# A DLRM forward pass: samples taken in pairs of 64-sample units, one unit in each half of the partitions, and which engine copies and which one fetches

## What is computed

```python
x = relu(dense_features @ W0 + b0)        # 13 -> 512
x = relu(x @ W1 + b1)                     # 512 -> 256
dense_out = relu(x @ W2 + b2)             # 256 -> 64
emb = tables[f, sparse_features[:, f]]    # (2048, 26, 64)
gram = einsum('bid,bjd->bij', emb, emb)
interact = gram[:, TRIU_I, TRIU_J]        # 325 products for each sample
y = concatenate([dense_out, interact], 1) @ Wt + bt   # 389 -> 256
```

## Time and profile before

| | before |
|---|---|
| time, median of 3 runs | 537.5 us (534.24, 537.5, 538.75) |
| profiled execution, its own time | 535.61 us |
| its span, first to last instruction | 533.8 us |
| PE busy (matmuls) | 345.1 us, 65% |
| DVE busy | 206.8 us, 39% |
| ACT busy | 203.7 us, 38% |
| POOL busy | 389.7 us, 73% |
| gathers on POOL | 407, 956 ns each |
| mean granted TensorE clock | 0.76 of full speed |

### The profile page before, as it was taken

The page is one execution under the profiler, slowest core; times in us unless marked ns, Lnnn a source line. Parts: engine busy times, 40 slices in busy tenths (PEclk is TensorE's granted clock), DMA queues, the critical chain, the costliest instruction groups (busy, mean ns, idle before and its releaser), DMA issues.

```text
span 533.8 us, 8006 instructions
## 1 busy us (share of the span) xinstructions
PE 345.1 (65%) x1744; PEld 285.4 (53%) x1744; DVE 206.8 (39%) x648; ACT 203.7 (38%) x637; POOL 389.7 (73%) x414
## 2 busy tenths in 40 slices
PE   2067854895846965658747786369854487617975
PEld 1055743674635854537636665257643376516864
DVE  6432344334324343244443342432451425314353
ACT  2023444345224453144432452433541436313462
POOL 6777777777777777777777777777777777777760
PEclk9555887769767788677877697685895869757699
DMA  5214112221122212221212211222212221122110
GB/s 101 46 28 91 27 28 32 33 38 28 27 38 38 28 27 29 38 37 28 29 26 38 39 27 30 38 28 37 28 28 37 38 30 26 28 38 35 27 26 21
DMA packets 23182, 18.66 MB, mean 35 GB/s; under 512 B 12775, under 2 KB 16585, under 8 KB 23116
## 3 DMA queue, kind: packets, MB, share of 16 engines
q0 software_dynamic: 13024, 13.36, 17.8%
q1 hardware_dynamic: 6612, 2.52, 2.2%
q10 hardware_dynamic: 3498, 2.26, 1.4%
HBM read 15.20 MB, written 2.10 MB: 32 GB/s over the span
## 4 chain that ended last, share of the span: by engine, by line
POOL 72%; issue 23%; PE 1%; DVE 1%; DMA 1%; POOLq 0%
POOL emb L283 72%; PE mlp_ps L573 1%; DVE gram L198 1%; DMA emb<-in_L_rec_tables_dram,row_idx 1%; DMA raw_idx<-n_r_sparse_features_dram 0%; PE gram_ps L560 0%; POOLq L79 0%; PE rowsT_ps L543 0%; POOLq L278 0%; DVE out_sb L372 0%; DVE embT L184 0%; DVE wrap L313 0%; DVE row_idx L323 0%; DVE wrapped L317 0%; DVE capped L314 0%
## 5 line engine op out<-in xcount | busy, mean ns | idle before, releaser
L283 POOL DMA_INDIRECT emb<-in_L_rec_tables_dram,row_idx x407 | 388.9, 956 | 127.5 <-issue 123.8
L198 ACT COPY gram<-gram_ps 32x48 f32<-32x48 f32 (+1 forms) x512 | 122.9, 240 | 151.0 <-PE gram_ps L560 145.2
L198 DVE COPY gram<-gram_ps 32x48 f32<-32x48 f32 (+1 forms) x512 | 122.2, 239 | 124.6 <-PE gram_ps L560 117.7
L560 PEld LDWEIGHTS gram_ps<-embT 128*128 128x128 f32 x1024 | 144.5, 229 | 17.2 <-issue 9.4
L560 PE MATMUL gram_ps<-embT 128*128 128x100 f32 x1024 | 148.5, 312 | 4.1 <-DVE embT L184 4.1
L543 PE MATMUL rowsT_ps<-ident,emb 128*128 128x128 f32 (+1 forms) x215 | 49.5, 341 | 157.0 <-DMA emb<-in_L_rec_tables_dram,row_idx 135.6
L184 DVE COPY embT<-rowsT_ps 64x512 f32<-64x512 f32 (+2 forms) x96 | 65.0, 689 | 154.2 <-PE rowsT_ps L543 153.8
L543 PEld LDWEIGHTS rowsT_ps<-ident,emb 128*128 128x128 f32 (+1 forms) x215 | 28.1, 163 | 175.5 <-DMA emb<-in_L_rec_tables_dram,row_idx 129.8
L184 ACT COPY embT<-rowsT_ps 64x512 f32<-64x512 f32 x64 | 53.4, 861 | 109.1 <-PE rowsT_ps L543 108.6
L573 PE MATMUL mlp_ps<-w_gram,gram 128*128 128x256 f32 x224 | 72.3, 485 | 1.9 <-DVE gram L198 1.9
L573 PEld LDWEIGHTS mlp_ps<-w_gram,gram 128*128 128x128 f32 x224 | 57.3, 260 | 14.3 <-DVE gram L198 2.3
(11 more groups left out here) (28 smaller groups left out, 39.8 us busy)
## 6 DMA issues: line engine op xcount, KB each, us to landing
by_hand<-in_L_rec_tables_dram SPq DMA_DIRECT2D x1152, 0.2 KB
emb<-in_L_rec_tables_dram,row_idx POOLq DMA_INDIRECT x407, 2.7
out_dram<-out_sb ACTq DMA_DIRECT2D x16, 128.0 KB, 1.9
w_gram<-w_tri SPq DMA_DIRECT2D x3, 192.0 KB
w_sb<-in_L_rec_W_dram SPq DMA_DIRECT2D x1, 512.0 KB
raw_idx<-n_r_sparse_features_dram SPq DMA_DIRECT2D x2, 182.0 KB, 3.9
w_gram<-w_tri SPq DMA_DIRECT2D x1, 224.0 KB
x_sb<-in_r_dense_features_dram ACTq DMA_DIRECT2D x1, 104.0 KB, 2.8
```

Of the source, the lines that this page charges most:

```text
L198: last = copy(gram[FP * g:FP * (g + 1), q, t0:NS, c0 + a0 * SQ + s:c0 + a1 * SQ:SQ], gram_ps[FP * s:FP * (s + 1), a0:a1, src:src + SQ * (N ...
L283: nc.gpsimd.indirect_dma_start(emb[:, j, k, :], None, tables_v[:, :], bass.IndirectOffsetOnAxis(ap=row_idx[:, r * UR + j, k:k + 1], axis=0 ...
L560: last = nc.tensor.matmul(gram_ps[:, a, 0:SQ * (F - 1)], samples.rearrange("p s f -> p (s f)"), samples[:, :, 1:F], start=True, stop=True)
```

## The change

Two units are taken together as a pair: 16 pairs, two to a round (`ROUNDS` stays 8).

- A gathered tile holds a field pair of both units side by side (`emb[.., k, u, :]`), with room for three pairs (`PR`). A transpose then takes field pair k of both units, and leaves unit 0 in partitions 0 to 63 and unit 1 in 64 to 127. There are 13 transposes for a pair instead of 14, in four chunks.
- DVE makes every copy: to `embT` (four for a pair, over 128 partitions), all 16 block copies of a half pair (96 or 112 elements for each of 32 partitions), and the ReLUs of the MLP. ACT makes only half of the block copies of the last pair.
- `gram_products` contracts over 64 partitions, alternately the lower and the upper ones. A half of it has 16 matmuls (8 groups for each unit). `gram_ps` has the same size and is laid out by unit, so that both halves of a pair use the same place: the second half waits for the block copies of the first (`gram_ready`).
- `BY_HAND` names eight pairs; of each, field pair k=11 of both units is fetched by hand, unit 0 by SyncE and unit 1 by ACT, 128 DMAs each. ACT stores results between its fetches, at fixed places in the list of 32 pieces.
- SyncE fetches the first pair's rows ahead of the `w_tri` weights; the zeroing of `w_tri` comes after the index arithmetic on DVE, and `embT` is zeroed only where no field stands.
- In the last round the MLP's layers 1 and 2 and `top` of pair 14 are issued ahead of the transposes of pair 15.

```diff
+    PR = 3
+    ROUNDS = NP // 2
+    RS = 4 * US
...
-    CHUNKS = [range(0, 8), range(8, 12), range(12, NK)]
+    CHUNKS = [range(0, 4), range(4, 8), range(8, 12), range(12, NK)]
     LAST = len(CHUNKS) - 1
-    BANK = [0, 1, 1]
-    assert all(ks.start % 2 == 0 and ks.stop <= 8 * (bank + 1) for ks, bank in zip(CHUNKS, BANK))
...
-    BY_HAND = [4, 7, 10, 13, 16, 19, 22, 25, 28]
...
+    BY_HAND = [2, 4, 6, 8, 9, 11, 13, 15]
+    HAND_K = 11
...
+    def gathered(m, c):
+        return 2 * len([k for k in CHUNKS[c] if k != HAND_K or m not in BY_HAND])
+    def all_gathered(m, c):
+        return 16 * sum(gathered(i, c) for i in range(m % PR, m + 1, PR))
...
+        by_hand = sb("by_hand", [P, len(BY_HAND), 2, EMB])
...
+        emb = sb("emb", [P, PR, NK, 2, EMB])
...
-        gram_ps = pb("gram_ps", [P, NG, P])
+        gram_ps = pb("gram_ps", [P, 2, HG, P])
...
-        def rowsT_evac(copy, c, odd, j):
+        def rowsT_evac(copy, c, m):
             ks = CHUNKS[c]
-            i = (ks.start - 8 * BANK[c]) // 2
-            m = len(ks[odd::2])
-            dst = embT[0:EMB, j % 2, :, 0:F].rearrange("p s (k x) -> p k x s", x=2)
-            return copy(dst[:, ks.start + odd:ks.stop:2],
-                        rowsT_ps[BANK[c]][odd * EMB:(odd + 1) * EMB, i:i + m])
+            return copy(embT[:, m % 2, :, 0:F].rearrange("p s (k x) -> p k x s", x=2)[:, ks.start:ks.stop],
+                        rowsT_ps[c % 2][:, 0:len(ks)])
...
+        def gram_evac(copy, blocks, m, half):
+            by_quad = gram[:, m % 2, :, :].rearrange("p t (u a s) -> p t u a s", u=2, s=SQ)
             for s, g in blocks:
                 t0 = first_slot(g)
                 src = s * (F - 1) + col(t0, g) - 1
                 last = copy(
-                    gram[FP * g:FP * (g + 1), q, t0:NS, c0 + a0 * SQ + s:c0 + a1 * SQ:SQ],
-                    gram_ps[FP * s:FP * (s + 1), a0:a1, src:src + SQ * (NS - t0 - 1) + 1:SQ].rearrange("p a t -> p t a"))
+                    by_quad[FP * g:FP * (g + 1), t0:NS, :, half * HG:(half + 1) * HG, s],
+                    gram_ps[FP * s:FP * (s + 1), :, :, src:src + SQ * (NS - t0 - 1) + 1:SQ].rearrange(
+                        "p u a t -> p t u a"))
...
+            sp.wait_ge(hand_idx_ready, 1)
+            fetch_rows(sp, 0, BY_HAND[0], 0, P)
             sp.wait_ge(tri_zeroed, 1)
...
-            for i in range(1, len(BY_HAND)):
-                fetch_rows(i, 0, P)
+            for m in BY_HAND[1:]:
+                fetch_rows(sp, 0, m, 0, P)
...
+            def gather(m):
+                wait_if_any(pool, rowsT_in_psum[LAST], m + 1 - PR)
+                if m == FIRST // 2:
                     pool.wait_ge(later_ready, 1)
...
+                        if k == HAND_K and m in BY_HAND:
+                            continue
+                        for u in range(2):
+                            nc.gpsimd.indirect_dma_start(
+                                emb[:, m % PR, k, u, :], None, tables_v[:, :],
+                                bass.IndirectOffsetOnAxis(ap=row_idx[:, 2 * m + u, k:k + 1], axis=0),
+                            ).then_inc(rows_in[m % PR][c], 16)
...
-                if part == 1:
-                    nc.vector.memset(w_tri[:, :, :], 0.0).then_inc(tri_zeroed, 1)
...
-            nc.vector.memset(embT[:, :, :, :], 0.0)
+            nc.vector.memset(embT[:, :, :, F:FP], 0.0)
             nc.vector.memset(gram[:, :, 0, :], 0.0)
             nc.vector.memset(h2[H2:H2 + 1, :], 1.0).then_inc(consts_set, 1)
+            nc.vector.memset(w_tri[:, :, :], 0.0).then_inc(tri_zeroed, 1)
...
+            def embT_evac(m):
+                wait_if_any(dve, gram_in_psum, (m - 1) * 2)
                 for c in range(len(CHUNKS)):
+                    dve.wait_ge(rowsT_in_psum[c], m + 1)
+                    rowsT_evac(nc.vector.tensor_copy, c, m).then_inc(embT_ready[c], 1)
+            def gram_blocks(m, half):
+                wait_if_any(dve, top_in_psum[m % 2], m // 2)
+                dve.wait_ge(gram_in_psum, 2 * m + half + 1)
+                if m < LAST_PAIR:
+                    gram_evac(nc.vector.tensor_copy, BLOCKS, m, half).then_inc(gram_ready, 1)
+                else:
+                    gram_evac(nc.vector.tensor_copy, DVE_BLOCKS, m, half).then_inc(gram_tail_dve, 1)
...
+            def relu(out, in_, bias):
+                return nc.vector.tensor_scalar(out, in_, bias, 0.0, ALU.add, ALU.max)
...
+            def vector_round(r):
+                embT_evac(2 * r)
+                gram_blocks(2 * r, 0)
+                if r > 0:
+                    out_evac(2 * r - 1)
+                gram_blocks(2 * r, 1)
+                l0_evac(r)
+                if r < ROUNDS - 1:
+                    embT_evac(2 * r + 1)
+                    gram_blocks(2 * r + 1, 0)
+                    l1_evac(r)
+                    gram_blocks(2 * r + 1, 1)
+                    l2_evac(r)
+                    out_evac(2 * r)
+                else:
+                    l1_evac(r)
+                    l2_evac(r)
+                    out_evac(2 * r)
+                    embT_evac(2 * r + 1)
+                    gram_blocks(2 * r + 1, 0)
+                    gram_blocks(2 * r + 1, 1)
...
+            pieces = [(m, c0) for m in BY_HAND for c0 in range(0, P, LOADED)]
+            act.wait_ge(hand_idx_ready, 1)
+            for i, (m, c0) in enumerate(pieces):
+                for done in range(LAST_PAIR):
+                    if done * 7 // 3 + 6 == i:
+                        store(done)
+                fetch_rows(act, 1, m, c0, c0 + LOADED)
+            for done in range(LAST_PAIR):
+                if done * 7 // 3 + 6 >= len(pieces):
+                    store(done)
+            act.wait_ge(top_in_psum[LAST_PAIR % 2], LAST_PAIR // 2)
+            for half in range(2):
+                act.wait_ge(gram_in_psum, LAST_PAIR * 2 + half + 1)
+                gram_evac(nc.scalar.copy, ACT_BLOCKS, LAST_PAIR, half).then_inc(gram_tail_act, 1)
+            store(LAST_PAIR)
...
+            def transposes(m):
+                for c, ks in enumerate(CHUNKS):
+                    pe.wait_ge(rows_in[m % PR][c], all_gathered(m, c))
+                    own = HAND_K in ks and m in BY_HAND
                     if own:
-                        pe.wait_ge(by_hand_in[BY_HAND.index(n)], 16 * P)
...
+                        for u in range(2):
+                            pe.wait_ge(by_hand_in[BY_HAND.index(m)][u], 16 * P)
+                    wait_if_any(pe, embT_ready[(c + 2) % 4], m if c < 2 else m + 1)
+                    nc.tensor.nop(nofuse=True)
+                    for k in ks:
+                        rows = by_hand[:, BY_HAND.index(m), :, :] if own and k == HAND_K else emb[:, m % PR, k, :, :]
+                        last = nc.tensor.transpose(rowsT_ps[c % 2][:, k - ks.start, :, :],
+                                                   rows.rearrange("p u e -> p (u e)"), ident[:, :])
                     last.then_inc(rowsT_in_psum[c], 1)
...
+            def gram_products(m, half):
+                if m == LAST_PAIR and half == 1:
+                    pe.wait_ge(gram_tail_dve, 1)
+                    pe.wait_ge(gram_tail_act, 1)
+                else:
+                    wait_if_any(pe, gram_ready, 2 * m + half)
+                pe.wait_ge(embT_ready[LAST], m + 1)
+                nc.tensor.nop(nofuse=True)
+                for a in range(HG):
+                    for u in range(2):
+                        at = (half * HG + a) * SQ
+                        samples = embT[u * EMB:(u + 1) * EMB, m % 2, at:at + SQ, :]
+                        last = nc.tensor.matmul(gram_ps[:, u, a, 0:SQ * (F - 1)], samples.rearrange("p s f -> p (s f)"),
                                                 samples[:, :, 1:F], start=True, stop=True)
-                    last.then_inc(gram_in_psum, 1)
...
+            def tensor_round(r):
+                transposes(2 * r)
+                gram_products(2 * r, 0)
+                if r > 0:
+                    top(2 * r - 1)
+                gram_products(2 * r, 1)
                 mlp_l0(r)
+                if r < ROUNDS - 1:
+                    transposes(2 * r + 1)
+                    gram_products(2 * r + 1, 0)
+                    mlp_l1(r)
+                    gram_products(2 * r + 1, 1)
+                    mlp_l2(r)
+                    if r == 0:
+                        pe.wait_ge(w_top_in, 96)
+                        pe.wait_ge(tri_zeroed, 1)
+                    top(2 * r)
+                else:
+                    mlp_l1(r)
+                    mlp_l2(r)
+                    top(2 * r)
+                    transposes(2 * r + 1)
+                    gram_products(2 * r + 1, 0)
+                    gram_products(2 * r + 1, 1)
```

More of the change, by code:

```diff
@@ L606, in _ @@
+            for r in range(ROUNDS):
                 tensor_round(r)
-            top(ROUNDS - 1, 1)
+            top(LAST_PAIR)
 _INS = ['r_dense_features', 'r_sparse_features', 'L0_rec_tables', 'L0_rec_W0', 'L0_rec_b0', 'L0_rec_W1',
```

257 lines of the change are left out of this document (64 added, 193 removed).

## The result

| | before | after |
|---|---|---|
| time, median of 8 runs each | 537.39 us (534.24 to 538.88) | 541.68 us (540.17 to 542.16) |
| ratio to before, 95% interval | | 1.0084 [1.0059, 1.0108] |
| profiled execution: time, span | 535.61, 533.8 us | 541.29, 539.5 us |
| start of the last gather, S | 517.06 us | 504.26 us |
| from there to the end of the span | 16.7 us | 35.2 us |

The change costs 0.8%: clear of the noise by the interval, and under the 1% that the forecast took as the smallest difference. The forecast was 537.9 us, from 532 to 547, with "within 1%" as the likeliest. Span against span it was 5.3 us short (534.2), and that is the sum of two errors of opposite sign.

What follows compares the result with a forecast made beforehand. POOL's queue of gathers was taken to bound the kernel: seven fewer gave -8.7 us, a longer tail +9.1, so the span went from 533.8 to 534.2 and the time from 537.5 to 537.9 us; 80% range 532 to 547.

Steps and rivals of the forecast that it cites:

- products(14): Tail: pair 14's first products on PE start at S-26.4, after landing 2.7 us and transpose and copy 0.85.
- Seven fewer gathers, POOL never waits: POOL's queue: 400 gathers instead of 407, one every 1.2486 us without stalls, so -8.7 us.
- Rival 4: Start: the w_tri memset holds the second gather (5.34 us); moving it could free 4.4 us, giving 533.5; chance 0.05.
- Fetches by hand cost 0: SP and ACT queues: 1024 DMAs each, SP 400 us, ACT done near 450 us, before pair 15 needs them.
- Rival 5: Fetch queues: ACT's fetches late, or more DMAs stretching each gather by 1% (+5 us); chance 0.05.
- Engine work fits in the middle of the run: PE and DVE mid-run: a pair's chain of 22 to 30 us is covered by the gathers, at no cost.
- Blocks at 317 and 347 ns: DVE's block copies: 317 ns for 96 elements, 347 for 112; sixteen take 5.4 us.
- Products: A half's 16 matmuls (32 passes) on PE: neighbours overlap, 2.3 us at full clock and 4.0 at half.
- Rival 1: Products on PE don't overlap: +7.4 us in the tail, 545.3 us; chance 0.22.
- The clock: PE in the tail: pair 14's first products at half clock after waiting, second at full; layer 1 slowed to 5.5 us.
- rival 2: PE's clock stays at 1.2 GHz through the tail because DVE's turns leave it idle: +13, 551 us; chance 0.08.
- Rival 3: Tail: pair 14's work ends before pair 15's last rows land; products start 5.45 us earlier, 532.4 us; chance 0.12.

Runs made afterwards that it cites:

- a_act_no_fetch: The changed kernel with ACT fetching nothing and POOL gathering unit 1's rows instead (408 gathers): 542.54 us, 1.0095 of the kernel before.
- a_same_round: The changed kernel with pair 15's transposes and first products ahead of layers 1 and 2, as in other rounds: 534.76 us, 0.9983 of the kernel before.

## Why the forecast was near, and which steps failed

Span against span, forecast and trace:

| step | forecast | trace | difference |
|---|---|---|---|
| start of the last gather, S | 508.3 | 504.26 | -4.1 |
| products(14) | S-26.4 | S-18.2 | +8.2 |
| products(14) to products(15) | 35.4 | 33.9 | -1.5 |
| products(15) to the end | 16.9 | 19.55 | +2.7 |
| span | 534.2 | 539.5 | +5.3 |

- **Seven fewer gathers, POOL never waits**: right. 400 gathers, 945 ns each, still one per 1.249 us.
- **Rival 4, the zeroing holds a gather up** (chance 0.05): it came true, with 4.1 us where it named 4.4. The step that failed is the argument against it, "gathers beside the 3.47 us memset of `embT` take 0.94". That row was true and was about a memset with nothing but memsets behind it; I compared the instruction that ran and not the queue behind it. The other half of the argument, that the moved memset would fall on a gather again, failed for the same reason.
- **Fetches by hand cost 0**: this step failed, for 8.2 us. I asked only whether they would be done in time. They were: ACT ended at 460 us (forecast: near 450), and their rows are not on the chain. What they did to the gathers' landing I took from the earlier trace rows, 2.7 us, which is the landing beside one fetching queue. Rival 5 named "more DMAs beside the gathers" but as 1% of a gather's duration; the duration stayed at 0.94 and the longest landing was six times 2.7.
- **Engine work fits in the middle of the run**: right there, and for the reason given. It is why the delay costs nothing until the last pairs.
- **Blocks at 317 and 347 ns**: right, by form they took 317 and 347. Sixteen took 5.37 to 5.43 us (5.4 forecast). The ReLUs: four in 1.66 (1.75). Layer 1: 5.65 (5.5), at a partly halved clock as argued.
- **Products**: 2.3 and 4.0 were priced near the lower bound, and the bound was it, 2.03 and 3.73. Rival 1 fell. (From these bounds full overlap is 1.7 us less in the tail, 0.5 and three times 0.4, and not 1.5.)
- **The clock**: pair 14's first products ran at full clock and not at half, since the late start put them right behind other PE work (0.82 us idle): -2.0. In `a_act_no_fetch`, where pair 14 isn't late, they took 3.74 behind waits of 5.01 and 1.40 us. The last products ran at half clock and the last `top` for the most part, +1.4 and +1.8, which is a piece of rival 2. The windows (us, busy of PE, PEld, DVE, ACT and POOL, granted clock, DMA share, GB/s):

```profile
519.00:525.00 6.00, 2.03 (x32) 1.89 (x32) 3.39 (x10) 2.54 (x8) 0.00 (x0) 1.00 0.01 3
525.00:535.00 10.00, 8.17 (x42) 6.67 (x43) 2.59 (x8) 2.61 (x9) 0.00 (x0) 0.51 0.01 2
```

  The second burst stands behind 3.13 us of idle and got 1.2 GHz. My evidence against rival 2 were gaps of up to 1.94 us; the change's own gap is longer, because both DVE and ACT copy eight blocks of twice the size between the bursts.
- **Rival 3, the last pair isn't held up**: no, but `a_same_round` shows that the order of the last round alone holds it up.

So it was luck that the number came so near: two steps failed and partly cancel. Without the delayed landing, and with the rest of the trace as it is, the span would be 539.5 - 8.2 = 531.3 us by estimate, 0.5% under that of before.

## What to carry to other kernels

When a second queue begins to issue many small DMAs, look at the landing of the transfers that others wait for, over the whole run and at its end, and not only at whether the new queue finishes in time: here the mean share of the DMA engines stayed under a third. When an instruction is moved, compare what stands behind it in its queue at both places. Work at the end of a run should not depend on a queue that is only just done: with one pair fewer by hand the last gather started 2.9 us later, and the kernel was 7 us faster.

## What the hardware showed that was not expected

- A gather on GpSimd beside a DVE memset takes 0.94 us, but one that a `tensor_scalar` between SBUF tiles next in DVE's queue holds takes 1.58 to 6.62 us; it ends about 1 us after the memset.
- Two queues that each issue a 256-byte DMA every 0.39 us delay the completion of 128-row gathers by up to 13.5 us, at a mean DMA share of 0.28. With SyncE's queue alone (`a_act_no_fetch`) the landings of the same stretch are 2.4 to 3.4 us.
- At full clock, 32 passes of 64 rows take 3.45 us in one half of the array and 2.03 us in alternate halves; over 128 rows 3.81. The Trainium skill, "TensorE: Matmul & The Clock Gate", section "Part 3: Packing small matmuls — row/col tiling", says that such matmuls run concurrently, and the trace agrees.
